# Scores of the first attention as products of 32-row strips, with an order of PE, DVE and ACT written anew around them

## What is computed

```python
def _L0_xattn_ref(q, latent_kv, Wq, Wkv_expand, Wout):   # q = layernorm(x): (32, 100, 256); latent_kv: (32, 1444, 64)
    H, NH = 256, 16; HD = 16
    qp = q @ Wq.T
    k, v = jnp.split(latent_kv @ Wkv_expand.T, 2, axis=-1)
    # 16 heads of 16 columns
    scores = jnp.einsum('bhqd,bhkd->bhqk', qh, kh) / 4
    scores = jnp.where(causal, scores, finfo.min)
    attn = jax.nn.softmax(scores, axis=-1)
    out = jnp.einsum('bhqk,bhkd->bhqd', attn, vh)
    return out @ Wout.T
x = x + jnp.tanh(g_xattn[0]) * _L0_xattn_ref(_layernorm(x), ctx_512, ...)
```

## Time and profile before

| | |
|---|---|
| median of three runs | 3296.32 us (3287.39 to 3297.56) |
| the profiled execution | 3302.86 us, its span 3301.1 us |
| first attention in it | from the start to 446.5 us |
| first score maximum of group 0 | 43.75 us |
| first score maximum of group 7 | 401.40 us |
| PE, DVE, ACT busy, 42 to 93 us (about one group) | 48.4, 38.4, 16.3 us of 51 |

### The profile page before, as it was taken

The page is one execution under the profiler, slowest core; times in us unless marked ns, Lnnn a source line. Parts: engine busy times, 40 slices in busy tenths (PEclk is TensorE's granted clock), DMA queues, the critical chain, the costliest instruction groups (busy, mean ns, idle before and its releaser), DMA issues. The chain is left out here.

```text
span 3301.1 us, 62826 instructions
## 1 busy us (share of the span) xinstructions
PE 2836.6 (86%) x18352; PEld 1917.0 (58%) x18352; DVE 2270.5 (69%) x4122; ACT 1658.6 (50%) x3458; POOL 1637.5 (50%) x1196
## 2 busy tenths in 40 slices
PE   5999979999798998898998999899899899886335
PEld 4777769999665565565555555556556556553123
DVE  5777764454376686677677667768767667766887
ACT  2333222222146646646646655655664664664556
POOL 0000012322166656666666666665665666663566
PEclk9888879999899999999999999999999999998566
DMA  4000010000300101000000000010110000011100
GB/s 112 0 0 0 0 48 10 5 10 10 75 6 21 26 10 23 19 16 17 21 21 16 22 19 17 16 26 7 23 23 11 22 19 16 11 48 35 44 13 24
DMA packets 130264, 71.20 MB, mean 22 GB/s; under 512 B 83582, under 2 KB 124510, under 8 KB 129880
## 3 DMA queue, kind: packets, MB, share of 16 engines
q1 hardware_dynamic: 129944, 67.45, 8.2%
HBM read 56.95 MB, written 10.04 MB: 20 GB/s over the span
## 5 line engine op out<-in xcount | busy, mean ns | idle before, releaser
L1194 POOL TENSOR_TENSOR c_psum<-c_p 120x800 f32<-120x800 f32 (+1 forms) x384 | 770.8, 2013 | 558.8 <-ACT c_p L1508 240.1
L1508 ACT ACTIVATE c_p<-c_s_ps 120x400 f32<-120x400 f32 (+1 forms) x1536 | 650.5, 512 | 331.8 <-PE c_s_ps L1680 258.7
L1692 PE MATMUL c_o_ps<-c_p,c_val 120*64 120x400 f32 (+1 forms) x3072 | 605.1, 516 | 10.9 <-ACT c_onum L1473 10.9
L1271 DVE TENSOR_REDUCE c_mpart<-c_m_ps 128x1 f32<-128x484 f32 x416 | 271.4, 653 | 203.6 <-PE c_m_ps L1587 203.1
L1587 PE MATMUL c_m_ps<-c_kmax,c_q 64*128 64x484 f32 x1080 | 308.5, 437 | 98.6 <-DVE c_mpart L1271 63.6
L1316 DVE TENSOR_TENSOR c_acc<-c_acc,c_psum 120x800 f32<-120x800 f32 x256 | 319.3, 1247 | 59.9 <-POOL c_psum L1194 57.9
L1185 POOL TENSOR_TENSOR l_rr<-c_psum,l_rr 96x400 f32<-96x400 f32 x256 | 263.6, 1052 | 191.0 <-DVE l_rr L1338 190.9
L1692 PEld LDWEIGHTS c_o_ps<-c_p,c_val 120*64 120x64 f32 (+1 forms) x3072 | 188.8, 137 | 273.5 <-issue 159.7
L1676 PE MATMUL c_s_ps<-c_q,c_k 64*120 64x400 f32 (+1 forms) x1536 | 322.9, 370 | 1.8 <-ACT c_p L1508 1.8
L1623 PE MATMUL c_s_ps<-c_xt,l_a 128*96 128x400 f32 x1536 | 310.8, 352 | 9.7 <-DVE l_rr L1338 7.8
L1277 DVE CUSTOM_DVE_ANT_0 c_xt<-c_m_ps,c_xt,c_mpart 128x484 fp32r<-128x484 f32 x360 | 259.9, 722 | 86.0 <-DVE c_mpart L1271 42.1
(11 more groups left out here) (258 smaller groups left out, 5212.1 us busy)
## 6 DMA issues: line engine op xcount, KB each, us to landing
c_rdb<-l_denominators SPq DMA_DIRECT2D x128, 100.0 KB, 2.7
c_kv<-in_ctx SPq DMA_DIRECT2D x32, 360.0 KB
c_mrow<-c_mneg SPq DMA_DIRECT2D x288, 0.5 KB, 2.0
x_rows<-in_x SPq DMA_DIRECT2D x4, 800.0 KB
x_spill<-x_rows SPq DMA_DIRECT2D x8, 400.0 KB
l_xa<-x_spill SPq DMA_DIRECT2D x8, 400.0 KB
c_xr<-x_spill SPq DMA_DIRECT2D x32, 100.0 KB
x_spill<-c_xr SPq DMA_DIRECT2D x32, 100.0 KB
```

What stands on the lines that cost most here:

```text
L1194: g.tensor_tensor(psum[0:k, u % 2, :], p[0:k, 2 * u % 4, :], p[0:k, (2 * u + 1) % 4, :], ALU.add).then_inc(psum_ready, 1)
L1271: v.tensor_reduce(mpart[:, t:t + 1], m_ps[:, bank, 0:4 * KP], AX.X, ALU.max, negate=True).then_inc(mpart_ready, 1)
L1508: a.activation(p[0:k, w % 4, i * HALFQ:(i + 1) * HALFQ], s_ps[0:k, (2 * w + i) % 4, 0:HALFQ], ACT.Exp).then_inc(exp_ready, 1)
L1692: mm = pe.matmul(o_ps[i * DL:(i + 1) * DL, 0:HALFQ], val[0:k, j % 2, r, :], p[0:k, w % 4, i * HALFQ:(i + 1) * HALFQ], start=(r == 0), stop ...
```

## The change

- **Strips.** `block_keys`, `kt` and the head selector go. The evacuation of a key step writes `kbd` for the whole group: two products with a column of ones and zeros (`parity`: even heads, odd heads). A strip of 32 rows holds two heads; the scores of quarter q come from rows 32q to 32q + 31 of `qt` against the same rows of `kbd`, 200 columns for each k in 0, 1. A batch has eight such fp32 products, k outermost, so the four quarters of one k lie next to each other, in different rows and banks. The mask products are issued apart (`place_mask`) and counted by `mask_done`, on which `scores` waits for all four. A quarter now holds heads 8k + 2q + e.
- **Order on PE.** In batch b: bank 0, turning 0, bank 1, turning 1, values 0, bank 2, bank 3, scores of batch b + 1, turning 2, values 1, `turn_out(b - 1)`, turning 3, values 2, `project_out(b - 1)`, values 3. "Bank q" waits for the differences of batch b, quarter q, and places the mask of the next batch there, or, in the group's last batch, is a dense step of the next group.
- **Products that nobody reads.** `keep_busy` is an fp32 product of 100 rows and 256 columns. One stands before the masks of quarters 1 and 2, one before the turnings of quarters 0 and 1, and two before each of the dense steps 0 to 2.
- **Dense steps** are reordered: latents, rows 0, rows 1, keys 0, keys 1, queries 0, values 0, values 1, queries 1.
- **Evacuations.** ACT takes keys 0 and both values; DVE the rest. Those of the rows stand behind the last batch's four differences, that of the latents behind its first.
- **DVE order.** `normalise(b - 1)` and `add_x(b - 2)` stand between quarters 1 and 2 of batch b; row statistics and normalised rows at the end of batches 0 and 1. In the eighth group `split_moe` stands ahead of `add_x(2)` and `normalise(3)`.

```diff
+                    elif n == KEYS1:
+                        for e in range(2):
+                            ins = v.tensor_scalar(kbd[:, 1, e, :], src, parity[:, e:e + 1], None, ALU.mult)
+                        ins.then_inc(vec_out, 1)
...
+                def keep_busy(bank):
+                    pe.matmul(bank[0:S, 0:D], m.ident[0:S, 0:S], lat[:, 0:D], start=True, stop=True)
...
+                    if n < KEYS0:
+                        for i in range(2):
+                            keep_busy(s_ps[:, n % 4, :])
...
+                def scores(it, b):
+                    pe.wait_ge(mask_done, PRIMED + (it * G + b + 1) * NQ)
+                    pe.sem_inc(m.carrier, 1)
+                    for k in range(KT):
+                        for q in range(NQ):
+                            rows = slice(32 * q, 32 * (q + 1))
+                            mm = pe.matmul(s_ps[0:S, q, 2 * k * S:2 * (k + 1) * S], qt[rows, k, b * S:(b + 1) * S],
+                                           kbd[rows, k, :, b * S:(b + 1) * S], start=False, stop=True, skip_group_check=True)
+                            if k == KT - 1:
+                                mm.then_inc(s_ready, 1)
...
+                def next_bank(b, q):
+                        if b + 1 < G:
+                            pe.wait_ge(diff_ready, PRIMED + (it * G + b) * NQ + q + 1)
+                            if q in FILL_MASKS:
+                                keep_busy(s_ps[:, q, :])
+                            place_mask(q)
+                        elif more:
+                            dense(it + 1, q)
...
+                        for q in range(NQ):
+                            differences(b, q)
+                            if b == G - 1 and more and q == 0:
+                                evacuate(it + 1, LATENTS)
+                            if q == 1 and b > 0:
+                                normalise(b - 1)
+                            if q == 1 and b > 1:
+                                add_x(b - 2)
+                        if b == 0 and more:
+                            row_stats(it + 1)
+                        if b == 1 and more:
+                            normalise_rows(it + 1)
                     if more:
-                        for k in range(7, ND):
-                            evacuate(it + 1, k)
+                        evacuate(it + 1, ROWS0)
+                        evacuate(it + 1, ROWS1)
+                        evacuate(it + 1, KEYS1)
+                        evacuate(it + 1, QUERIES0)
+                    else:
+                        split_moe()
+                    add_x(G - 2)
+                    normalise(G - 1)
+                    if more:
+                        evacuate(it + 1, QUERIES1)
                     add_x(G - 1)
```

More of the change, by code:

```diff
@@ L106, in phase_l0_attention @@
         qt = sb("a_qt", [128, KT, T])
-        kt = sb("a_kt", [128, KT, T])
-        kbd = [sb(f"a_kbd{i}", [128, KT, 8, S]) for i in range(2)]
+        kbd = sb("a_kbd", [128, KT, 2, T])
         va = sb("a_va", [S, G, H, HD + 1])
@@ L306, in _, with evacuate, group @@
             def _(a):
-                with a.Fori(0, NG) as it:
+                def evacuate(it, n):
+                    a.wait_ge(dense_mm, PRIMED + it * ND + n + 1)
+                    a.sem_inc(m.carrier, 1)
+                    if n == KEYS0:
+                        for e in range(2):
+                            ins = a.activation(kbd[:, 0, e, :], s_ps[:, n % 4, 0:T], ACT.Copy, scale=parity[:, e:e + 1])
+                    else:
+                        for j in range(2):
+                            ins = a.activation(va[:, 2 * (n - VALUES0) + j, :, 0:HD],
+                                               s_ps[0:S, n % 4, j * D:(j + 1) * D].rearrange("p (h d) -> p h d", h=H), ACT.Copy)
+                    ins.then_inc(act_out, 1)
+                def group(it, more):
                     def copy_ct(b):
@@ new lines, in first_scores @@
+                def first_scores(it):
+                    vec_done(it, QUERIES0)
+                    place_mask(1)
+                    act_done(it, VALUES0)
+                    place_mask(2)
+                    act_done(it, VALUES1)
+                    place_mask(3)
+                    vec_done(it, QUERIES1)
+                    place_mask(0)
+                    act_done(it, KEYS0)
+                    vec_done(it, KEYS1)
+                    scores(it, 0)
+                def group(it, more):
@@ L438, in group @@
                     if more:
-                        for k in range(7, ND):
-                            dense(it + 1, k)
+                        dense(it + 1, VALUES1)
                     turn_out(G - 1)
+                    if more:
+                        dense(it + 1, QUERIES1)
                     project_out(G - 1)
+                    if more:
+                        first_scores(it + 1)
                 for k in range(ND):
                     dense(0, k)
+                first_scores(0)
```

243 lines of the change are left out of this document (116 added, 127 removed).

## The result

The kernel with the change takes **3371.65 us** (median of six runs, 3345.58 to 3421.96), the kernel before on the same chip 3291.21 (3284.51 to 3297.56). The ratio is 1.0202, 95% interval 1.0162 to 1.0242: slower by 2%, where I had forecast 3280 and given 3308 as the upper end. The ratio is over the four runs within 1.5% of the fastest (median 3357.5 us, 14 under the median of all six), since two, the profiled one among them, took 3421 us at a lower clock.

What follows compares the result with a forecast made beforehand. PE was taken to set the pace, slowed by stretches at 1.2 GHz. Seven groups at 49.3 against 51.1 us, -4.4 ahead of group 0 and +0.6 for the eighth gave -16.4: about 3280 us, range 3250 to 3308.

Steps and rivals of the forecast that it cites:

- the clock: PE in each group: one fall to 1.2 GHz of some 2 us, 1.0 us lost, giving 49.3 us a group.
- The strips: PE's eight fp32 score products a batch take 1.5 us, bounds 0.68 and 2.7, plus 0.1 for leaving the strips.
- A group at full clock: One group at 2.4 GHz, four batches summed: 48.3 us, 2 to 3 more than the 45 to 46 before.
- the wait at a group's start: PE in batch 0 waits for the first difference, in all 0.9 us idle.
- Batch 2: Third batch of a group, with a turned output and a projection added: 9.3 us, PE full again.
- The new wait behind the latents: PE in batch 3 idles 1.7 us for difference 1, as DVE first waits for and splits the latents.
- An idle product: A product nobody reads on PE costs 0.43 us; 20 a group, 8.6 us.
- the gain must come from the clock: Whole group: 2 to 3 us more PE time at the same clock, so any gain comes from less clock loss.
- Ahead of group 0: Before the first group: first maximum at 39.3 instead of 43.75, so -4.4 us, bounds -3 and -5.5.
- The eighth group: Last group, ending in `split_moe`: 45.7 us against 45.1 before, +0.6.
- Rival 1: Strips abreast and clock held: 0.68 us scores a batch, 45.1 a group, total 3248 (3261 with 0.9 scores and loss); chance 0.18.
- Rival 3: Clock falls as before: 2.8 us lost a group gives 3292 (chance 0.20), 5.6 gives 3313 (chance 0.10).

Runs made afterwards that it cites:

- e4: Kernel before, with score products reading 64 of the 128 rows (the other rows' block keys are zero): 3548.33 us, 1.0769 of the kernel before.
- e3: Changed kernel without any idle products: 3396.83 us, 1.0306 of the kernel before.
- e5: e3 with block keys on DVE and four 128-row score products in place of the strip products: 3374.73 us, 1.0225 of the kernel before.
- e13: e2 with idle products of 68 rows in place of 100, same columns: 3532.23 us, 1.0733 of the kernel before.
- e15: Changed kernel with idle products of 128 rows and 128 weight columns, streaming part of Wout, same number and places: 3277.36 us, 0.9942 of the kernel before.
- e2: Changed kernel with an idle product ahead of all four turnings, so six a batch: 3309.60 us, 1.0045 of the kernel before.
- e6: Changed kernel with strip products ordered quarter by quarter, so a quarter's two products follow each other: 3321.36 us, 1.0086 of the kernel before.
- e12: e2 with idle products of 32 rows in place of 100, same columns: 3627.21 us, 1.1016 of the kernel before.
- e14: e2 with idle products of 64 rows in place of 100, same columns: 3628.07 us, 1.1021 of the kernel before.
- e1: Changed kernel with the idle products of turnings 0 and 1 moved ahead of turnings 2 and 3, behind the scores: 3484.24 us, 1.0601 of the kernel before.
- e17: Changed kernel with three full-array idle products a batch, ahead of turnings 0, 2 and 3: 3374.32 us, 1.0239 of the kernel before.

## Why the prediction was wrong

**The step that failed is the clock.** I wrote: "I take one fall of some 2 us a group, 1.0 lost: 49.3". Lost were 20 us a group (120.4 / 6) in the profiled execution. I had read the falls of before as the work of a wait and of short products, and looked in the new order for waits. The runs put this in its place: with columns and order equal, PE's clock went with the rows at work in its array. Strips took 2.7 us of 128-row products out of every batch and put 0.87 us there, in which four products of 32 rows run abreast; four idle products of 100 rows a batch did not make up for it. e4 shows it in the kernel before (64 rows instead of 128: 1.0769), e3 and e5 in the new order (0.58 and 0.85), e13 and e15 on the idle products alone (in e13 68 rows against e2's 100, six a batch; in e15 128 rows and columns against the change's 100, four a batch). The most direct are e4 and e13, which change rows alone, e4 with the height. PE is then busy for 70 of 73 us and slow, so no view of busy time or waits shows it. That the clock falls is shown to go with rows; that it falls behind short products, and at times behind a wait, as I had read it in before, the traces of the change show too, and no run changed columns or waits alone.
The Trainium skill, TensorE: Matmul & The Clock Gate, What's actually happening, describes the gate as following how busy PE has been. By busy time alone the trace disagrees: 70.42 of 73.22 us busy gave 0.63, and in e15 44.07 of 47.44 gave 1.00.

**The strips.** I took 1.5 us a batch, on "if records start in order, the second record of a strip blocks the queue". The term was mis-sized: 0.87, near the lower bound, and e6 shows that the reason fails. 2.7 / 0.87 = 3.1 times.
The Trainium skill, TensorE: Matmul & The Clock Gate, Measured speedup vs the span model, gives 3.07 for four row tiles at 512 columns; the trace agrees, and shows it for fp32 products of 200 columns.

**A group at full clock** was right where the clock was. The forecast was 48.3; with 0.87 for the scores four times it would be 48.3 - 4 x 0.63 = 45.8; e15 has 47.43, so terms of 1.6 were missing. One is the wait at a group's start (predicted 0.9, measured 1.23, below); the rest I have not placed. That 48.3 and 47.4 lie so close is in part luck: the strips were too dear and other terms too cheap. Batch 2: 9.3, or 8.7 with 0.87; measured 8.80. The new wait behind the latents: 1.7; measured 1.55 (e15). An idle product: 0.43; e2 has eight more a group than e15, 3.44 us by that price, and its group is 50.81 - 47.44 = 3.37 longer. So "the gain must come from the clock" held too: at full clock the new group, 47.4, is no shorter than before's best window, 47.73 at 0.96 or 45.8 by the same measure as above. What e15 wins, it wins by holding 1.00 where before lost 6 us a group.

**Ahead of group 0.** I forecast a first maximum at 39.3 in place of 43.75. Measured is 44.06. The timelines of after:

```profile
36.66 2.88 PE L389 MATMUL a_s_ps<-a_wv,a_latt 64*100 64x256 f32 x12
...
43.14 0.94 PE L410 MATMUL a_s_ps<-a_kbd,a_qt 32*100 32x200 f32 x16 [0.26 <-PE a_s_ps L401]
...
45.30 0.37 PE L401 MATMUL a_s_ps<-a_mask,a_identb 100*100 100x400 bf16 x1 [1.23 <-DVE a_diff L231]
```

```profile
44.06 0.57 DVE L227 TENSOR_REDUCE a_mx<-a_s_ps 100x4 f32<-100x400 f32 x1 [1.61 <-PE a_s_ps L410]
```

I had put PE at 2.4 GHz from 32.9 on ("Then, at 2.4 GHz, queries 0 to 34.2"). The twelve value products take 2.88 at 36.66, where the same twelve took 1.67 at full clock: PE was still slow. The keys and both query steps took 2.37 each. What the block keys gave back, the clock took.

**The eighth group.** From `split_moe` to the end I had 9.4 + 1.05 + 3.6 = 14.05 us. After has 554.93 to 568.98, 14.05:

```profile
554.93 1.62 DVE L278 CAST l_a<-raw_weights 128x2816 fp32r<-128x2816 f32 x1
...
568.50 0.48 DVE L245 SCALAR_TENSOR_TENSOR x_rows<-a_f_ps,tanh_gates,x_rows 100x256 f32<-100x256 f32 x1 [3.14 <-PE a_f_ps L440]
```

The terms of the whole group add up to 45.85, not to the 45.7 that I wrote.

**The rivals.** No rival was right as it stood. Rival 1 was right in its first half (strips abreast) and wrong in its second. Rival 3 (the clock falls as before, with "3.7 us of short value products in a row") was right in kind, with 0.10 for its slower end, and far too small: it took the loss of before (5.6) as the most that the clock could cost. That is where the range went wrong. The most was to be had from the rows I had: a group of 45 us of PE work at 1.2 GHz throughout is near 90 by estimate, and the windows of e4 (80 to 83), e12 and e14 (90 to 97) come near it. Had I let the upper end of the clock's term stand for "slow throughout", the range would have reached over 3500.

**Still open**: what part the wait at a group's start and the short products behind the scores have in a fall, and with it why the idle products do worse behind the scores (e1); why the strips quarter by quarter hold the clock better (e6); and why three full ones do not suffice (e17) where four do. The change's own spread over 76 us from run to run suggests that it stands near an edge, where small things decide.

## What to carry to other kernels

Where PE sets the pace, ask of every product that is made shorter in rows what the array does instead: a product over the whole array may be half wasted zeros and still be what holds the clock, and the price of losing it is up to the whole of PE's work again. If idle products are used at all, try them over the full array: the same number in the same places cost 80 to 94 us more with 100 rows and columns than with 128, and no other form beat the kernel before. And a range for the clock reaches to "slow throughout" as soon as the change touches what PE has in its array.

## What was not expected of the hardware

- The granted clock went with the rows of the idle products, streamed columns being equal: six of 32, 64, 68 and 100 rows a batch gave 3627, 3628, 3532 and 3310 us, at 0.56, 0.56, 0.58 to 0.61 and 1.00 in most groups; four of 100 rows and columns gave 3372, four of 128 rows and columns 3277.
- Sixteen fp32 records in four strips start over 0.87 to 0.89 us, 0.054 to 0.056 each, whichever order they have (e6).
- The clock column reads 1.00 in stretches near the start in which products take twice their time (e2's strips at 54.40, and e12's as late as 94.11, 1.67 us): there only durations tell.
- Changes of PE's height seem to cost by themselves: 64 instead of 68 rows, 3628 against 3532 us and 1.10 against 0.85 us an idle product at 1.2 GHz, part of which may be the four rows.
- A fall lasts: in the change's seventh group the clock stayed at 1.2 GHz from 448.4 to 503 with PE busy for nearly all of it, and came back behind query products over the whole array.
